# Sixteen input jobs of the setup stage, dealt over the first ten rows of the adjacency instead of the first twelve

## The reference

```python
HW = layernorm(x) @ W                          # (8, 2048, 128)
A_norm = relu((A + A.T) * 0.5)                 # (2048, 2048), symmetric
d = sum(A_norm, axis=1) ** -0.5                # 0 where the sum is 0
x = x + relu((eye - d[:, None] * A_norm * d[None, :]) @ HW)
x = x + moe(layernorm(x))                      # 8 experts, the two best of each token, gelu
```

## Time and profile before

| what | value |
|---|---|
| median of three executions | 886.82 us |
| the profiled execution, its own time | 886.36 us |
| its span | 884.6 us |
| mean granted clock of TensorE over the span | 0.984 |
| PE busy, share of the span | 845.1 us, 96% |
| DVE busy, share | 639.1 us, 72% |
| ACT busy, share | 478.5 us, 54% |
| POOL busy, share | 301.0 us, 34% |
| chain that ended last, by engine | PE 88%, DVE 5%, ACT 3%, issue 2%, DMA 1% |

### The profile page before, as it was taken

The page is one execution under the profiler, slowest core; times in us unless marked ns, Lnnn a source line. Parts: engine busy times, 40 slices in busy tenths (PEclk is TensorE's granted clock), DMA queues, the critical chain, the costliest instruction groups (busy, mean ns, idle before and its releaser), DMA issues.

```text
span 884.6 us, 14390 instructions
## 1 busy us (share of the span) xinstructions
PE 845.1 (96%) x4098; PEld 703.2 (80%) x4098; DVE 639.1 (72%) x1557; ACT 478.5 (54%) x872; POOL 301.0 (34%) x311
## 2 busy tenths in 40 slices
PE   3688999999999999999999999999999999999996
PEld 3687788888888888888888777888888888888884
DVE  3678644578898644343425589999999999999995
ACT  2687423224333210111111588888888888888885
POOL 1893253574757444555444610010000000000001
PEclk9996999999999999999999999999999999999999
DMA  9994376686765257977778765677777777777771
GB/s 281 322 313 143 123 273 251 226 286 246 261 227 189 83 198 272 322 287 275 258 267 329 298 247 198 261 280 285 289 282 270 259 273 270 269 288 272 273 289 48
DMA packets 93006, 222.98 MB, mean 252 GB/s; under 512 B 8888, under 2 KB 59600, under 8 KB 81056
## 3 DMA queue, kind: packets, MB, share of 16 engines
q1 hardware_dynamic: 87760, 212.96, 68.0%
q0 software_dynamic: 2688, 8.59, 2.5%
q10 hardware_dynamic: 2512, 0.86, 0.4%
HBM read 157.89 MB, written 64.49 MB: 251 GB/s over the span
## 4 chain that ended last, share of the span: by engine, by line
PE 88%; DVE 5%; ACT 3%; issue 2%; DMA 1%; ACTq 0%; DVEq 0%; POOL 0%; POOLq 0%
PE bank L956 13%; PE bank L958 13%; PE bank L957 13%; PE bank L1372 6%; PE bank L1356 6%; PE bank L1358 6%; PE bank L1357 6%; PE bank L1369 6%; PE bank L1370 6%; PE bank L342 3%; PE bank L893 2%; PE bank L1378 2%; PE bank L323 1%; PE bank L446 1%; ACT s_tri L605 1%
## 5 line engine op out<-in xcount | busy, mean ns | idle before, releaser
L1408 ACT ACTIVATE act_h<-bank,b_sb 128x512 f32<-128x512 f32 x256 | 176.6, 690 | 46.8 <-PE bank L1358 43.4
L1446 DVE TENSOR_TENSOR gated<-c_all,act_h 128x512 f32<-128x512 f32 x256 | 177.6, 694 | 28.6 <-ACT act_h L1408 20.9
L1451 DVE TENSOR_TENSOR g_lo<-gated,g_hi 128x512 fp32r<-128x512 f32 x256 | 175.6, 686 | 0.2
L1415 ACT ACTIVATE g_hi<-gated 128x512 fp32r<-128x512 f32 x256 | 159.3, 622 | 4.9 <-DVE gated L1446 4.9
L1339 POOL DMA_DIRECT2D out<-fin x32 | 24.3, 760 | 343.3 <-DVE fin L1459 332.1
L1025 POOL TENSOR_SCALAR z<-x,mv,rstd 128x128 f32<-128x128 f32 x128 | 106.6, 846 | 3.4
L956 PE MATMUL bank<-y_hi,stage 128*128 128x512 f32 x256 | 105.6, 413 | 1.6 <-DVE y_lo L732 0.9
L1356 PE MATMUL bank<-z_e,w_hi 128*128 128x512 f32 x256 | 103.4, 404 | 2.6 <-ACT act_h L1408 2.5
L978 ACT ACTIVATE z_hl<-bank 128x512 fp32r<-128x512 f32 x32 | 19.1, 598 | 155.3 <-PE bank L893 155.3
L1372 PE MATMUL bank<-g_lo,w_hi 128*128 128x512 f32 x256 | 101.1, 395 | 0.9 <-DVE g_lo L1451 0.7
L956 PE MATMUL bank<-y,stage 128*128 128x512 f32 x256 | 101.2, 395 | 0.0
(11 more groups left out here) (127 smaller groups left out, 1474.8 us busy)
## 6 DMA issues: line engine op xcount, KB each, us to landing
c_all<-c_scratch SPq DMA_DIRECT2D x64, 1024.0 KB, 8.0
s_scratch<-stage SPq DMA_DIRECT2D x14, 2048.0 KB, 8.2
stage<-s_scratch SPq DMA_DIRECT2D x14, 2048.0 KB, 8.0
z_e<-z_scratch SPq DMA_DIRECT2D x32, 512.0 KB, 7.0
z_scratch<-z_hl SPq DMA_DIRECT2D x31, 512.0 KB, 2.7
x_raw<-in_x SPq DMA_DIRECT2D x32, 256.0 KB, 6.7
x_res<-in_x SPq DMA_DIRECT2D x32, 256.0 KB, 7.1
r_e<-res_scratch SPq DMA_DIRECT2D x32, 256.0 KB, 2.7
```

The lines of the kernel that those rows point to most:

```text
L1408: act.activation(v.act_h[e % R][:, :], ps_h[e % 2][:, :], ACT.Gelu, bias=v.b1_sb[:, e:e + 1]).then_inc(gelu_done, 1)
L1415: act.activation(v.g_hi[e % R][:, :], v.gated[e % R][:, :], ACT.Copy).then_inc(hi_done, 1)
L1446: dve.tensor_tensor(out=v.gated[e % R][:, :], in0=v.c_all[s][:, e, :], in1=v.act_h[e % R][:, :], op=ALU.mult).then_inc(gated_done, 1)
L1451: dve.tensor_tensor(out=v.g_lo[e % R][:, :], in0=v.gated[e % R][:, :], in1=v.g_hi[e % R][:, :].bitcast(FP32), op=ALU.subtract).then_inc(lo ...
```

## The change

The sixteen jobs are dealt over the rows in another way: two to each of rows 0 to 5 and one to each of rows 6 to 9, where it was two to each of rows 0 to 3 and one to each of rows 4 to 11.

```diff
-    JOBS = [2, 2, 2, 2, 1, 1, 1, 1, 1, 1, 1, 1, 0, 0, 0, 0]
+    JOBS = [2, 2, 2, 2, 2, 2, 1, 1, 1, 1, 0, 0, 0, 0, 0, 0]
```

## The result

Six executions of the changed kernel took 889.23 to 893.56 us, median 891.38 us; six of the kernel before had a median of 886.18 us. The ratio is 1.0055, with a 95% interval of 1.0041 to 1.0070: about 4.9 us slower. The same kernel measured again beside later experiments gave 1.0069 (1.0056 to 1.0082). The profiled execution took 891.2 us with a span of 889.5 us, 4.9 us more than before.

A forecast was written before the change was run, and what follows sets the result against it. Loads, PE-ACT hand-overs, then DVE's tail were taken as limits in turn. Row 9's 6.3 us delay, less mainly 3.2 us of statistics, left the last add 2.6 us late: 889.0 us, 889.4 against the median, range 886.4 to 892.2.

The forecast's parts named there:

- My sum: Whole kernel: row delays less what the tail gives back put the last column add, and so the end, 2.6 us late.
- the clock's 2 us: Rows 5 and 6: longer waits may drop PE to half clock there as well, costing 0 to 2 us more.
- The rival with the loads as the limit: Loads set the end: no row after row 9 moves, tail 3.2 us shorter, 883.6 us, faster; chance 0.1.
- I take 1.88: Row 4: from transposes to the row's first block, product between, 1.88 us at half clock; row begins at 46.78 us.
- The step before it: Row 4: from job 8's `copy_x` at 44.14 us to the next transposes 0.76 us, giving 44.90 us.
- the 3.2 us of the sum: DVE's tail: two sets of statistics, 1.76 and 1.43 us, no longer fall there, giving back 3.2 us.
- POOL's wait: Tail: DVE's next column add, ready at 74.6 us, waits some 0.35 us for POOL's last column add.
- I count most as gone: Tail: of 0.8 us of gaps before 76.41 us most vanish, as the turned rows lie ready.
- The third rival: Clock falls again or loads run late: two more rows at half clock, dry queue reaching row 14; 891.5 us, chance 0.2.
- my case: Whole kernel: slower, 889.4 us, with the last add 2.6 us late; chance 0.5.
- The rule of the Trainium skill: PE's clock: granted clock follows how busy PE has lately been; longer idle stretches put the change near 891 us.
- The other one: Skill rule to improve the most contended engine first, DMA read by utilisation: DMA is the limit, the faster case follows.

The follow-up runs named there:

- the filled tail: The changed kernel with two more sets of statistics on DVE at rows 10 and 11, results unread: 894.94 us, ratio 1.0104 to the kernel before.
- the second bank: The changed kernel with the odd jobs' transposes of x going to a second PSUM bank: 887.69 us, ratio 1.0015 to the kernel before.
- the kernel with late loads: The changed kernel with only SP's loads of x dealt as in the kernel before: 894.76 us, ratio 1.0102 to the kernel before.
- fewer constants than 18: The run made had 18 products of constants on PE in rows 4 and 5 of the changed kernel: 892.67 us, ratio 1.0077 to the kernel before.
- early statistics and loads alone: The kernel before with only SP's loads of x and DVE's statistics dealt as in the change: 884.14 us, ratio 0.9983.
- the first experiment: Half of the change, only row 4 doubled against the kernel before (jobs two to rows 0 to 4, one to rows 5 to 10): 889.55 us, ratio 1.0037.
- the fastest kernel: The kernel before with early statistics and loads, and a second PSUM bank for transposes of odd jobs 1 to 13: 883.51 us, ratio 0.9974.

## Why the prediction was right, and where its size was off

**Right: the side, the mechanism and the range.** The forecast was slower, 889.4 us in 886.4 to 892.2; measured 891.38. My sum had 2.6 us, measured are 4.9 (3.6 to 6.2), so the sum's size was too small by nearly half. The range held because it was wider than its reasons: half of the sum lost gives 888.1 us and the clock's 2 us give 891.4, not 886.4 and 892.2; the median lies on the edge of that narrower range. The rival with the loads as the limit is refuted: the queue was dry in 58 to 60 us and no row waited.

**Row 4: a duration was read wrong.** "I take 1.88" was the term: from transposes to the row at half clock, read from 46.96 to 48.84 us. The clock was back at full for the last 0.8 us of that, as the stretch of the kernel before beside that of the earlier trace rows from 48 us on shows:

```profile
46.00:48.00 2.00, 2.00 (x12) 2.00 (x11) 1.77 (x5) 1.74 (x5) 0.87 (x1) 0.50 1.08 322
```

Almost wholly at half clock it took 2.50 us (45.58 to 48.08). The step before it, 0.76 us to the transposes, held: 44.90 us predicted, 45.58 less 0.66 measured. Row 4 was 3.1 us late, not 2.4.

**Row 5: the clock fell once more.** I had it at full, with 0 to 2 us as bounds for further spells. It fell in 52 to 56 us, and the product before the second transposes took 1.83 us (53.02 to 54.85) instead of 0.97, so PE and not `copy_x` held them back, by 0.3 us, and from there to the row it took 1.86 us (54.85 to 56.71), not 1.36. Together that is near 0.9 us; rows 4 and 5 together were 7.2 us late, not 5.7. In the repeat of the change row 5's clock stayed up, and from row 4 to row 5 it took 7.80 us in place of 8.63.

**Rows 6 to 9: as worked out.** Row 6 followed row 5 by 5.33 us (5.4 predicted), row 7 by 2.60 (2.7), row 9 by another 6.53 (6.5). The 1.5 us were carried along unchanged.

**The tail: one term held, one did not.** The statistics came back in full: row 9's add to row 11's went from 7.40 us in the earlier trace rows to about 4.2 us (71.81 to 76.0), the 3.2 us of the sum, and the filled tail shows that four fifths of such time count at the end (2.0 of 2.5 us). POOL's wait was 0.32 us, predicted 0.35. But "I count most as gone" of the 0.8 us of gaps was wrong: the one before row 14 is 0.92 us, after 0.51 us before. The turned row does not lie ready, since the product of job 15 stands ahead of it on PE at half clock, in both kernels. The change, and the kernel before:

```profile
78.57 2.05 PE L342 MATMUL bank<-gnn_w_sb,x_t 128*128 128x128 f32 x8
80.42 0.42 PE L654 MATMUL bank<-ident,up 128*128 128x128 f32 x1
```

```profile
72.89 2.06 PE L342 MATMUL bank<-gnn_w_sb,x_t 128*128 128x128 f32 x8
```

At full clock such a product takes 1.06 us. The term is off by 0.9 us.

Together: 2.6 + 1.5 + 0.9 = 5.0 us at the last column add; with the 0.66 us by which the first rows happened to be later, 5.7 us, where 5.68 were measured. Of these the span shows 4.9. What follows the start of the last column add took 808.2 us before and 807.4 us in the change, and between 807.1 and 809.7 us in the fourteen profiles, so the 0.8 us lie within what differs from one to the next.

**The third rival,** with 891.5 us and a chance of 0.2, came nearer to the median than my case, and half by luck. Of its two further rows at half clock the profiled execution had one, the dry queue did not reach row 14, and the other 1.5 us that my sum lacked at the last column add came from row 4's duration and row 14's gap, which this rival did not name. The rule of the Trainium skill that the prediction named (TensorE: Matmul & The Clock Gate, Part 1) gave near 891 us, and the measured median stands there; the fall in row 5 behind PE's 2.35 us wait agrees with it, but that fall is 0.9 us of the 2.4 us lacking. The other one (Perfetto Trace Analysis, Identifying the Most-Contended Engine) pointed at the DMA engines, and the trace does not bear it out here: they were the busiest by share from 10 to 68 us in the kernel before (1.00 to 1.13 in stretches of 10 us), and yet the hand-overs between PE and ACT set the pace, with DVE behind.

What stays open: how the gain of the second bank divides between bank and clock, how the loss in the kernel with late loads divides between loads and clock, and whether fewer constants than 18, fitted to the wait, would gain.

## What to carry to other kernels

When small jobs are interleaved with big ones over several engines, each engine may have a dealing of its own: here early statistics and loads alone were worth 1.5 us, and with PE and ACT moved along the change lost 4.9, so that their part cost over 6. A second job in one slot costs more than its own work. In a double row at full clock 2.88 us passed between the wait for a `keep` and the row, in a single one 0.97 us (43.40 to 44.37); of the difference 0.45 us is the hand-over through the one bank and the rest the job's own transposes and product, and behind a double row comes the wait for its first `keep`, 2.4 us. So look for the engine's program order behind the wait (relus, keeps, copy): a further buffer for one hand-over only renames the wait at the next. Loads may be dealt ahead of their users only as far as the buffers they reuse are freed in time.

## What the runs showed of the hardware

**Which row meets the half clock is a matter of the execution.** One program up to row 9, three profiles: half clock from row 3 on in rows 4 and 5 (the change), in row 4 alone (its repeat), in rows 3, 5 and 6 (the filled tail). Each fall came in or behind a wait of PE for a `keep`, 1.9 to 2.4 us long, but not each such wait brought one. At about 1 us a spell this may make a good part of the spread within a kernel, 889.23 to 893.56 us for the change; no run shows that it does.

**A few of DVE's instructions wait out POOL's column add.** The small instruction L719 in the degrees took 1.09 us before and 1.07 us after, where the same line takes 0.17 us on five columns. In the kernel before it ended with POOL's column add, and in the first experiment, where it took 1.96 us, too (70.96 and 70.93 us). DVE and POOL of the kernel before:

```profile
64.85 1.09 DVE L719 TENSOR_SCALAR deg_none<-deg_raw 128x8 f32<-128x8 f32 x1
...
82.48 0.17 DVE L719 TENSOR_SCALAR deg_none<-deg_raw 128x5 f32<-128x5 f32 x1
```

```profile
63.77 2.12 POOL L570 TENSOR_TENSOR col_sum<-col_sum,s_tri 128x896 f32<-128x896 f32 x1
```

POOL's instruction ends at 65.89 us, DVE's at 65.94. In the fastest kernel the degrees missed POOL's add, and the next instruction, L424, met another (64.90 to 66.71 us) and took 1.89 us, to 66.85. It is a price of 0.9 to 1.8 us in a tail that DVE bounds. The Trainium skill, SBUF — State Buffer, Who interferes with whom, says that DVE in some of its modes, or with two inputs in SBUF, shares a pair of ports with GpSimd (POOL), and that the first to come holds it for its whole instruction. The rows of the long column adds agree. Beside POOL's small L296 (65.82 to 66.87 us in the kernel before) DVE's L721 and L724 took their usual 0.17 us.
